# Expert places scattered to a table during the projection, in place of a one-hot inversion; projection inputs loaded ahead

## The reference

```python
h = x + _attention(_rmsnorm(x, ln1_w), wq, wk, wv, wo)
# _moe, on xf = _rmsnorm(h, ln2_w)
logits = xf @ gate_w.T                     # 8 experts
rw, sel = jax.lax.top_k(logits, 2)
rw = softmax(rw)
for e in range(8):
    we = sum(where(sel == e, rw, 0.0), axis=-1)
    hh = silu(xf @ w1[e].T) * (xf @ w3[e].T)        # 512 wide
    out = out + hh @ w2[e].T * we[:, None]
```

## Time and profile before

| | |
|---|---|
| median of 3 runs | 3277.74 us (3275.07 to 3281.41) |
| the profiled execution's own time | 3278.61 us |
| its span | 3276.9 us |
| busy in the span | PE 88%, DVE 71%, ACT 58%, PEld 55%, POOL 19% |
| linear attention and projections | 0 to 794 us |
| softmax attention | 794 to 2140 us |
| output projection and gate | 2140 to 2315 us |
| route and transposed weights | 2315 to 2446 us |
| experts | 2446 to 3184 us |
| combine | 3184 to 3277 us |

### The profile page before, as it was taken

How to read it: one execution, slowest core, us unless ns; L and a number is a source line. 1 busy time by engine, 2 the same in 40 slices (tenths; PEclk the granted TensorE clock), 3 DMA queues, 4 the chain that set the end, 5 groups by cost and what they waited for, 6 DMA issues and landing times. The chain is left out here.

```text
span 3276.9 us, 64323 instructions
## 1 busy us (share of the span) xinstructions
PE 2891.2 (88%) x22812; PEld 1808.9 (55%) x22813; DVE 2334.1 (71%) x3783; ACT 1884.4 (58%) x3407; POOL 616.5 (19%) x983
## 2 busy tenths in 40 slices
PE   5888888884999999999999999969569999999970
PEld 4666677663333333333333333347458888888860
DVE  5676666763999999999999999646774444444436
ACT  3555565550688888888888888813233333333320
POOL 1122212121000000000000000011233444444430
PEclk8889988996899999999999999978789999999985
DMA  1323323323122222222222222168321111111129
GB/s 36 116 85 100 115 102 115 114 81 113 56 67 67 67 67 67 72 70 69 70 72 68 67 67 67 45 208 302 97 89 42 51 50 50 51 50 50 50 76 371
DMA packets 191429, 292.58 MB, mean 89 GB/s; under 512 B 31976, under 2 KB 118272, under 8 KB 191248
## 3 DMA queue, kind: packets, MB, share of 16 engines
q1 hardware_dynamic: 147184, 212.38, 20.7%
q0 software_dynamic: 18176, 52.45, 4.8%
q10 hardware_dynamic: 25888, 25.30, 2.3%
HBM read 159.94 MB, written 127.93 MB: 88 GB/s over the span
## 5 line engine op out<-in xcount | busy, mean ns | idle before, releaser
L819 DVE TENSOR_REDUCE b_mxq<-b_p_m 128x1 f32<-128x1024 f32 x1024 | 1222.3, 1223 | 72.1 <-PE b_p_m L841 65.1
L758 ACT ACTIVATE b_probs<-b_p_e 128x512 f32<-128x512 f32 x2048 | 1105.5, 597 | 148.4 <-PE b_p_e L889 39.8
L841 PE MATMUL b_p_m<-b_kst,b_qst 64*128 64x512 f32 x2048 | 765.5, 454 | 27.9 <-DMA b_vst<-v_d 23.7
L889 PE MATMUL b_p_e<-b_qst,b_kst 64*128 64x512 f32 x2048 | 747.8, 444 | 0.2 <-ACT b_probs L758 0.2
L860 PE MATMUL b_p_o<-b_probs,b_vst 128*32 128x256 f32 x8208 | 642.6, 390 | 0.5 <-ACT b_probs L758 0.4
L889 PEld LDWEIGHTS b_p_e<-b_qst,b_kst 64*128 64x128 f32 x2048 | 315.9, 184 | 419.7 <-ACT b_probs L758 355.3
L1489 ACT ACTIVATE d_act<-d_p_up 128x512 f32<-128x512 f32 x136 | 81.3, 597 | 486.8 <-PE d_p_up L1551 486.8
L841 PEld LDWEIGHTS b_p_m<-b_kst,b_qst 64*128 64x128 f32 x2048 | 320.0, 188 | 59.0 <-DVE b_mxq L819 30.9
L860 PEld LDWEIGHTS b_p_o<-b_probs,b_vst 128*32 128x32 f32 x8208 | 168.3, 108 | 324.4 <-issue 187.0
L1566 PE MATMUL d_p_y<-w2T,d_hT 128*128 x1096 | 258.7, 379 | 0.8 <-ACT d_hT L1483 0.8
L1504 DVE TENSOR_SCALAR d_xh<-d_p_x,d_ln 128x128 fp32r<-128x128 f32 x272 | 82.9, 346 | 238.0 <-PE d_p_x L1545 238.0
(11 more groups left out here) (267 smaller groups left out, 4026.1 us busy)
## 6 DMA issues: line engine op xcount, KB each, us to landing
b_qst<-qk_d SPq DMA_DIRECT2D x384, 64.0 KB
b_kst<-qk_d SPq DMA_DIRECT2D x384, 64.0 KB
x1y_d<-a_x1y SPq DMA_DIRECT2D x32, 512.0 KB, 4.2
qk_d<-a_hi SPq DMA_DIRECT2D x32, 512.0 KB, 2.8
qk_d<-a_lo SPq DMA_DIRECT2D x32, 512.0 KB, 3.7
v_d<-a_v_s SPq DMA_DIRECT2D x16, 1024.0 KB, 6.9
b_vst<-v_d SPq DMA_DIRECT2D x64, 256.0 KB
o_d<-b_oT POOLq DMA_DIRECT2D x64, 256.0 KB
```

What stands on the lines that cost most here:

```text
L758: nc.scalar.activation(probs[(2 * step + e % 4 // 2) % BUFS][:, (e % 2) * 512:(e % 2 + 1) * 512], p_e[(slot(e) if more1 else e) % EB][:], ...
L819: V_.reduce_max(mxq[half][:, h, qt:qt + 1], p_m[j % 2][:], AX.X).then_inc(s["m_red"], 1)
L841: mm(p_m[j % 2][:, kh * 512:(kh + 1) * 512], qst[r][rows(h), qt * P:(qt + 1) * P], kst[r][rows(h), kh * 512:(kh + 1) * 512], start=True, s ...
L889: mm(p_e[u % EB][:], kst[r][rows(h), kt * P:(kt + 1) * P], qst[r][rows(h), a * 512:(a + 1) * 512], start=True, stop=True).then_inc(s["e_ps ...
```

## The change

- Attention: the outputs `oT` are stored by SyncE's queue, between the 15 loads and the maxima of each pair, and no more by GpSimd. Behind the last pair SyncE loads the projection's weights (`load_weights`, 4 DMAs with the first `xy`), its first inputs and the first reciprocals, into tiles that outlive the stage (`ProjectionTiles`). GpSimd and VectorE make the identity and `heads` at the attention's start.
- Projection: the loads and constants at its start are gone. New for each half: VectorE compares the choices with the experts (`hot`), runs a sum over them that carries from half to half (`cum`), TensorE adds up over partitions (`p5`, two products of 64 columns), VectorE picks the place of each choice (`slot_i`), and GpSimd writes the choice's code to that place of a table in DRAM, by 8 indirect DMAs (`C` = 8) of 128 elements of 4 bytes. The table has 8 regions of 8192 places, and is filled with zeros at the stage's start. `count` runs one half behind, `place` two, the scatters three.
- Route: the running sums over all choices and the 128 one-hot columns are gone. A short chain of small operations computes which row of the table each tile is, two indirect DMAs gather them, and two transposes turn them. The weights' transposes have six PSUM banks, with a semaphore for each; ScalarE copies the rounded part, VectorE subtracts from PSUM, and GpSimd does none of it.

```diff
 # softmax_attention
+        def store(n):
+            sp.wait_ge(s["oT_done"], n + 1)
+            sp.dma_start(o_rows[n - 1], oT[n % 2][:]).then_inc(s[f"o_out{n % 2}"], 16)
...
             if more3:
                 sp.wait_ge(s["pv_done"], pair * KT + 2)
                 load(pair + 3, (r + 3) % RING)
+            if pair > 0:
+                store(pair)
             if more1:
                 maxima((r + 1) % 2, (r + 1) % RING, pair * SLOTS + (NEG_AT + 4))
...
         pairs(sp, body)
-        sp.wait_ge(s["o_stored"], 16 * (PAIRS - 8))
+        load_weights()
+        for k in range(2):
+            sp.wait_ge(s[f"o_out{k}"], 16 * (PAIRS - 8) // 2)
+        for half in range(2):
+            for k in range(2):
+                sp.dma_start(ahead.oin[half][:, k], ahead.o_rows(o_d)[0, half, 8 * k:8 * k + 8, 0:16, :]).then_inc(s["ahead_o"], 16)
         for n in range(BEFORE):
             sp.dma_start(den[:, n], ...).then_inc(s["den_in"], 16)
         sp.wait_ge(s["den_done"], 1)
...
         sp.wait_ge(s["den_out"], 32)
+        for half in range(2):
+            for k in range(2):
+                sp.dma_start(ahead.rd[half][16 * k:16 * k + 16, :].bitcast(f32), rd_d[k, 0, half]).then_inc(s["ahead_o"], 16)
+        store(PAIRS)
+        sp.wait_ge(s["ahead_w"], 64)
+        sp.wait_ge(s["ahead_o"], 128)
+        for k in range(2):
+            sp.wait_ge(s[f"o_out{k}"], 16 * PAIRS // 2)
...
 # gpsimd
         def body(pair, i, r, more1, more, more3):
-            pool.wait_ge(s["oT_done"], pair + 2)
-            g.dma_start(o_rows[pair], oT[(r + 1) % 2][:]).then_inc(s["o_stored"], 16)
             if more:
                 split(pair + 2, r % 2)
-            pool.wait_ge(s["o_stored"], pair * 16 + 16)
-            pool.sem_inc(s["o_free"], 1)

 # output_projection_and_gate, gpsimd
+        def scatter(n):
+            pool.wait_ge(s["slot_i_done"], n + 1)
+            for c in range(C):
+                g.indirect_dma_start(table_d, bass.IndirectOffsetOnAxis(ap=slot_i[n % 4][:, c:c + 1], axis=0), code[:, n * C + c:n * C + c + 1], None).then_inc(s[f"scat{n % 4}"], 16)
...
             g.tensor_tensor(r_s[:], r_s[:], mhalf[:], ALU.pow).then_inc(s["r_done"], 1)
+            if n > 2:
+                scatter(n - 3)
         halves(pool, body)
+        for n in range(N - 3, N):
+            scatter(n)
 # sync, at the end
+        for r in range(4):
+            sp.wait_ge(s[f"scat{r}"], 16 * C * N // 4)
 # vector
+        def count(n):
+            ...
+            V_.tensor_tensor(hot[r][:, :, 1:], chosen..., expert..., ALU.is_equal).then_inc(s["hot_done"], 1)
+            dve.wait_ge(s["hot_done"], 2 * n + 2)
+            V_.tensor_tensor_scan(cum[r]..., within..., hot[r]..., 0.0, ALU.mult, ALU.add).then_inc(s["cum_done"], 1)
+            dve.wait_ge(s["cum_done"], n + 1)
+            V_.tensor_copy(hot[1 - r][:, :, 0], cum[r][:, :, C]).then_inc(s["hot_done"], 1)
+        def place(n):
+            dve.wait_ge(s["slot_ps"], n + 1)
+            V_.tensor_tensor(where[:], p5[:], hot[r][:, :, 1:], ALU.mult).then_inc(s["where_done"], 1)
+            dve.wait_ge(s["where_done"], n + 1)
+            V_.reduce_sum(slot[:], where[:].rearrange("p e c -> p c e"), AX.X).then_inc(s["slot_done"], 1)
+            dve.wait_ge(s["slot_done"], n + 1)
+            V_.tensor_copy(slot_i[n % 4][:], slot[:]).then_inc(s["slot_i_done"], 1)
...
             if before:
                 choose(n - 1)
+            if n > 1:
+                place(n - 2)
+            if before:
+                count(n - 1)
             dve.wait_ge(s["r_done"], n1)
 # tensor
+            mm(p5[:], ones[:], cum[r][:, :, 0:C], start=True, stop=False)
+            mm(p5[:], lower[:], hot[r][:, :, 1:], start=False, stop=True).then_inc(s["slot_ps"], 1)

 # route (now tile_tables_and_weights), sync
                 if e > 0:
-                    sp.wait_ge(s["wT_ps"], 2 * (n - 2))
+                    sp.wait_ge(s[f"wT_ps{2 * j + 1}"], e)
                 sp.dma_start(raw[j]..., src).then_inc(s[f"raw_in{j}"], 16)
 # vector
-        with dve.Fori(0, C2 // 4) as i4:
-            ...
+        for e in range(NE):
+            rests(e)      # 4 subtractions PSUM - SBUF of 128x512, one copy of 128x512
+            if e == 3:
+                pick()
+            if e == 4:
+                tables()
```

More of the change, by code:

```diff
@@ L952, in output_projection_and_gate @@
     NT = 2 * n_batches * T
+    REGION = NT * P
+    C = 2 * T
+    i32 = mybir.dt.int32
+    ones, lower = sb("ones", [P, P]), sb("lower", [P, P])
+    zeros = sb("zeros", [P, NE * REGION // P])
+    expert_i, expert = sb("expert_i", [P, NE], i32), sb("expert", [P, NE])
+    code_i, code = sb("code_i", [P, 2 * NT], i32), sb("code", [P, 2 * NT])
+    within = sb("within", [P, NE, C + 1])
+    chosen = sb("chosen", [P, T, 2])
+    hot, cum = [sb(f"hot{r}", [P, NE, C + 1]) for r in range(2)], [sb(f"cum{r}", [P, NE, C + 1]) for r in range(2)]
+    where, slot, slot_i = sb("where", [P, NE, C]), sb("slot", [P, C]), [sb(f"slot_i{r}", [P, C], i32) for r in range(4)]
     best = sb("best", [P, NT, 2])
@@ L1011, in _ @@
         g = nc.gpsimd
[L1012 removed]
+        g.memset(zeros[:], 0.0).then_inc(s["zero"], 1)
         g.memset(mhalf[:], -0.5)
[L1014 to L1020 removed]
@@ L1021, in _ @@
[L1021 to L1028 removed]
+        g.memset(lower[:], 1.0)
@@ new lines, in _ @@
+        g.memset(within[:], 1.0)
+        g.iota(expert_i[:], [[1, NE]], base=0, channel_multiplier=0)
+        g.iota(code_i[:], [[2 * P, NT], [1, 2]], base=0, channel_multiplier=2).then_inc(s["iota_done"], 1)
+        pool.wait_ge(s["iota_done"], 1)
+        g.memset(within[:, :, 0], 0.0)
+        g.affine_select(out=lower[:], in_=lower[:], compare_op=ALU.is_gt, fill=0.0, base=0, pattern=[[1, P]], channel_multiplier=-1).then_inc(s["lower_done"], 1)
+        pool.wait_ge(s["code_done"], 1)
+        pool.wait_ge(s["zeroed"], 16)
@@ new lines, in tile_tables_and_weights @@
+    total, full, full_i, tiles, end = sb("total", [P, NE]), sb("full", [P, NE]), sb("full_i", [P, NE], i32), sb("tiles", [P, NE]), sb("end", [P, NE])
+    limit, skip, rise = sb("limit", [P, NE]), sb("skip", [P, NE]), sb("rise", [P, NE])
+    past, part = sb("past", [P, G, NE]), sb("part", [P, G, NE])
+    row, row_i, left = sb("row", [P, G]), sb("row_i", [P, G], i32), sb("left", [P, G])
+    cmp, ex = sb("cmp", [P, TILES, NE]), sb("ex", [P, TILES])
+    codes = [sb(f"codes{g}", [P, P]) for g in range(G)]
@@ L1282, in _ @@
-        g.affine_select(out=before[:], in_=before[:], compare_op=ALU.is_gt, fill=0.0, base=0, pattern=[[1, P]], channel_multiplier=-1).then_inc(s["pool"], 1)
-        for e in range(NE):
-            for j in range(4):
-                pool.wait_ge(s["wT_done"], e * 6 + j + 1)
-                lo = up_lo[:, e, j // 2, j % 2]
-                g.tensor_tensor(lo, lo.bitcast(f32), up_hi[:, e, j // 2, j % 2].bitcast(f32), ALU.subtract)
+        g_ = nc.gpsimd
+        g_.memset(ident[:], 0.0).then_inc(s["id0"], 1)
@@ new lines, in _ @@
+        V_.tensor_tensor(rise[:, 0:NE - 1], limit[:, 1:NE], limit[:, 0:NE - 1], ALU.subtract)
+        then(V_.tensor_tensor(past[:], mine[:].rearrange("p (g o) -> p g o", o=1).to_broadcast([P, G, NE]), end[:].rearrange("p (o e) -> p o e", o=1).to_broadcast([P, G, NE]), ALU.is_ge))
+        last = NE - 1
+        then(V_.tensor_tensor(part[:, :, 0:last], past[:, :, 0:last], skip[:].rearrange("p (o e) -> p o e", o=1)[:, :, 0:last].to_broadcast([P, G, last]), ALU.mult))
+        then(V_.reduce_sum(row[:], part[:, :, 0:last], AX.X))
@@ new lines, in _ @@
+        then(V_.tensor_tensor(row[:], row[:], mine[:], ALU.add))
+        then(V_.tensor_scalar(row[:], row[:], float(ROWS - 1), None, ALU.min))
+        V_.tensor_copy(row_i[:], row[:]).then_inc(s["row_done"], 1)
+        then(V_.tensor_tensor(part[:, :, 0:last], past[:, :, 0:last], rise[:].rearrange("p (o e) -> p o e", o=1)[:, :, 0:last].to_broadcast([P, G, last]), ALU.mult))
+        then(V_.reduce_sum(left[:], part[:, :, 0:last], AX.X))
+        then(V_.tensor_scalar(left[:], left[:], limit[:, 0:1], None, ALU.add))
@@ L1368, in _ @@
[L1368 to L1376 removed]
+        tr = nc.tensor.transpose
@@ L1379, in transposes @@
             for half in range(2):
-                if j or not isinstance(e, int):
-                    pe.wait_ge(s["wT_done"], e * 6 + (2 * j + half - 1))
+                b = 2 * j + half
+                if e > 0:
+                    pe.wait_ge(s[f"free{b}"], e)
                 for i in range(4):
```

392 lines of the change are left out of this document (209 added, 183 removed).

## The result

| | before | after |
|---|---|---|
| median | 3278.47 us (3275.07 to 3281.41, 4 runs) | 3370.82 us (3367.9 to 3373.28, 4 runs) |
| span of the profiled execution | 3276.9 us | 3366.2 us |
| ratio | | 1.028, interval 1.026 to 1.030 |

The forecast was 3244 us, its range 3222 to 3338. The result lies outside the range, on the other side.

What follows compares the result with a forecast made beforehand. VectorE's one-hot columns were taken to bound the route, with the projection already dense on DMA engines and TensorE. 3278.6 - 5.7 (handoff) + 49.0 (projection) - 78.3 (route) = 3244 us, range 3222 to 3338.

Steps and rivals of the forecast that it cites:

- part 2: Projection stage: added VectorE work, GpSimd's indirect DMAs and a longer tail were to cost +49 us.
- the slow rival: Projection: Rival (c), each scatter taking 1.8 us so that GpSimd bounds the stage; total 3336 us, chance 0.27.
- VectorE, 1.68 us for each half: Projection: 1.35 us of added operations and some 0.3 of waits, unhidden; half period 8.62 to 10.3 us, +20.2 over twelve.
- start-up halves: Projection's start, before the twelve periods: the added work was to cost +3 us.
- GpSimd's pitch, 1.0 us: Projection: indirect DMAs in a row take 1.0 us each, the 0.81 us of preparation hidden; ends 0.54 and 1.8.
- Rival (c): Projection: unrecorded 0.81 us is part of each DMA, period 15.9 us, GpSimd bounds it; total 3336 us, chance 0.27.
- Rival (b): Projection: VectorE's SBUF operations hold GpSimd 2.4 us per half, period 11.9, 19 us more; total 3263 us, chance 0.13.
- The tail, 38.7 us: Projection's end behind the last root: 32 scatters of 1.0 us, DRAIN, barrier and gaps; 38.7 for 12.9 us, +25.8.
- The route, 52 us, -78: Route stage: weight loads become the bound, eight rounds of 6.0 us plus 4; 52 us instead of 130.3, -78.3.
- Rival (a): Route: rounds take 7.5 us, with TensorE at 1.2 GHz and loads sharing the rate; 12 us back, 3256 us, chance 0.12.
- The handoff, -5.7: Attention to projection: with weights and inputs already in SBUF, transposes start at 2147.3 instead of 2153.0; 5.7 us saved.
- The experts unchanged: Experts and combination stages: same table sizes, costed at nothing.

## Why the prediction was wrong

**The step that failed** is the last sentence of part 2: "The 4-byte pieces load the DMA engines by an amount that no row shows; I take it as hidden, since the halves get longer; its upper bound is in the slow rival." It wasn't hidden, and no rival held it. It cost 87.5 us in the twelve periods (232.4 against 144.9 with the words apart) and 7.0 in the tail (52.6 against 45.6 with the table turned). Nor is it a load in the sense of that sentence: the pieces' own packets take 5.6 us of each engine's time, while the packets of the loads and stores beside them take 191 us instead of 96. Without these 94.5 us the change would have been at 3276, even with before. The slow rival gave a time for GpSimd's pitch, not for this; the range ended at 3338 because I had bounded the pieces by another cost. By the rule for what no row shows, it should have had two ends of its own. The rows to start from were there: the DMA engines were busy 87% already and VectorE was waiting for the stores, so a slowing of the DMA engines had little to hide behind.

The Trainium skill ("DMA: Bandwidth & Descriptors", "Specifications") says that transfers under 512 bytes make the DMA engine read, modify and write. I had not weighed it. By that rule alone all runs with single words should cost alike. They don't: words 512 bytes apart cost nothing that shows beside GpSimd's pitch, and neither do rows of 64 bytes. What the rule names, a read and a write of something larger than the piece, might explain why adjacent pieces hurt, but no run here shows what a DMA engine does with a line.

**Point by point.**
- *VectorE, 1.68 us for each half.* The six operations took 0.22 + 0.31 + 0.22 + 0.27 + 0.18 + 0.17 = 1.37 us; I had 1.35. But the period without scatters grew by 1.0 only (9.6 against 8.6), since VectorE had waits to fill. Mis-sized, +12 instead of +20. The start-up halves, forecast at +3, took 0.6 less.
- *GpSimd's pitch, 1.0 us.* It is 1.27, and the bound in the words-apart runs: 12.1 us for each period. This makes +29.6 (144.9 - 115.3). Bounds of 0.54 and 1.8 held it. I took the end nearer to the record; 0.30 of the unrecorded 0.81 us doesn't overlap.
- *Rival (c), pitch 1.8.* Wrong: 3336 lay nearest to the result, but by a mechanism that the trace refutes, with GpSimd waiting 88 us.
- *Rival (b), the shared port.* The mechanism is there, its size is not. I had VectorE holding GpSimd for `xg` and `base`, 2.4 us each half; with the table turned one scatter of a half is held, by `base`, for 0.45 us. The first scatter of a half, beside `xg`, takes 1.16 us, 0.2 more than the others; but the first behind the last root of the run with all scatters behind the halves took 1.23, almost all of it ahead of `xg`, so these 0.2 us are not shown to be `xg`'s. The Trainium skill ("SBUF — State Buffer", "Who interferes with whom") says that a VectorE instruction with two inputs in SBUF contends with a GpSimd instruction that reads SBUF. The trace agrees for `base`, which reads two operands from SBUF, in that the scatter beside it goes on when `base` ends; of 1.23 us only 0.45 are lost, since the scatter is due only when `base` is half done.
- *The tail, 38.7 us.* With real times 52.6: 32 x 1.27 = 40.6, then 12.1 from the last start to the route, of which the adjacent words account for 7 (with the table turned it is 5.0).
- *The route, 52 us, -78.* It took 56.2, -75.4. Loads landed in 4.5 us (median) and not 3.9; the bound is what I named, TensorE waits for `r_raw` 21.4 us. (3.9 was the median of all 24 loads before, not of one alone.) Rival (a) with its 64 us did not come. Right.
- *The handoff, -5.7.* -4.5 to the first root. SyncE's chain ran as worked out: sums from 2119.94 (2118.0 forecast, and the attention began 2.1 later), the stage's first load at 2150.54. GpSimd's DRAIN there fell from 5.28 us to 0.33. Right.
- *The experts unchanged.* +0.1 us. Right.

## What to carry to other kernels

Before small pieces are scattered to DRAM, look at where the 128 pieces of one DMA land: if they are neighbours of a few bytes, every store and load beside them pays. Turning the address (low bits to the top) cost here three more small operations of 0.17 us for each half, and 2 us in the route to pick the rows out of the turned table (58.0 against 56.2). A cost that no row shows gets bounds of its own, above all on a resource that is already near full. And what one engine has to issue in a dense stage may be able to stand in the next one, where it is idle; here it gained 1% twice, and once the loads beside it stalled for a reason not found.

## What the runs showed of the hardware

- Writes of adjacent words by one indirect DMA: the DMA engines are busy 85% at 128 GB/s, and 68% at 211 with the words apart. The scatters' own packets take 2.4% of the engines' time; those of the loads and stores take twice as long. Beside them a store of 512 KB kept ScalarE waiting for 22 us.
- Indirect DMAs in a row start 1.27 us apart, for 4 or 64 bytes a row, to adjacent or distant places; words gathered instead of scattered made the same period (144.7 us against 144.9).
- An indirect DMA that is due while VectorE adds two operands from SBUF goes on only as that ends (1.41 us in place of 0.96, in eleven of twelve periods).
- GpSimd's sequencer runs ahead of the records. Its row at the end of the projection starts at 2453.4, 14 us before the last scatter's record, so its 24.9 us are not a cost of their own:

```profile
L37 POOLq DRAIN  x1: 24928/24928/24928, 2453.4 to 2453.4; - x1
L37 SPq COMPARE_BRANCH  x1: 38/38/38, 2477.0 to 2477.0; - x1
```

SyncE, which waits for the landings, passes at 2477.0, and DRAIN ends at 2478.3. What sets the stage's end is the landing, 9.5 us behind the last scatter's start.
